# An MLP made layer by layer from seven half-size products, with its activations in DRAM

## What is computed

```
x: (8, 512, 512) fp32;  sa, ca, ga, sb, cb, gb = six rows of C = 512 per batch, from silu(c) @ wmod
h = layernorm(x) * (1 + ca) + sa
x = x + ga * attention(h)                 # 16 heads of 32, causal, W_attn and W_proj
h = layernorm(x) * (1 + cb) + sb
y = relu(h @ W1.T + b1)                   # 512 -> 1024
y = relu(y @ W2.T + b2)                   # 1024 -> 1024
x = x + gb * (y @ W3.T + b3)              # 1024 -> 512
```

## Time and profile before

| | |
|---|---|
| median of three runs | 1615.04 us |
| the profiled execution | 1619.41 us |
| its span, first to last instruction | 1617.6 us |
| attention, to the last matmul and store issue of it | 723.7 us |
| MLP | 893.9 us |
| busy: PE, DVE, ACT, POOL | 95%, 58%, 39%, 27% |
| DRAM traffic, mean | 73 GB/s |

### The profile page before, as it was taken

One profiled execution on the slowest core, in us unless ns is written; L12 is line 12 of the kernel. 1 busy time (PEld: TensorE's weight loads), 2 busy tenths in 40 slices (PEclk: granted clock), 3 DMA queues, 4 the chain that ended last, 5 costly groups with the idle time before them and its releaser, 6 DMA issues.

```text
span 1617.6 us, 31407 instructions
## 1 busy us (share of the span) xinstructions
PE 1540.7 (95%) x12112; PEld 1369.6 (85%) x12112; DVE 938.1 (58%) x2199; ACT 637.5 (39%) x1280; POOL 441.5 (27%) x459
## 2 busy tenths in 40 slices
PE   7899999999999999966899999999999999999998
PEld 6678788878888878855899999999999999999998
DVE  4477877787778777646644444444544444444442
ACT  2166666666666666654312121212121212121221
POOL 2156666666666666660000000000000000000000
PEclk9799999999999999987999999999999999999999
DMA  6534343434343433316201001110111011100100
GB/s 215 151 80 126 87 125 87 126 86 126 87 119 93 119 93 93 93 30 223 94 34 47 27 20 48 46 30 31 34 47 46 2 47 46 40 21 34 46 14 14
DMA packets 80546, 118.33 MB, mean 73 GB/s; under 512 B 10632, under 2 KB 31112, under 8 KB 80400
## 3 DMA queue, kind: packets, MB, share of 16 engines
q1 hardware_dynamic: 72416, 105.19, 24.1%
q10 hardware_dynamic: 7984, 11.03, 1.9%
HBM read 48.52 MB, written 16.81 MB: 40 GB/s over the span
## 4 chain that ended last, share of the span: by engine, by line
PE 52%; DVE 1%; DMA 1%; issue 0%; SPq 0%; ACT 0%; POOL 0%; DVEq 0%; POOLq 0%
PE feature L1268 34%; PE token L1249 17%; PE feature L1239 1%; PE token L1230 1%; DVE w L1180 1%; DMA b_rows<-b 0%; DMA w_ring<-wproj_t 0%; DVE y L1134 0%; SPq L1010 0%; DVE y L1132 0%; ACT w L1086 0%; DVE attn_tiles L1158 0%; POOL mlp_rstd L1047 0%; DVE gated L1170 0%; DVE res_tiles L1145 0%
## 5 line engine op out<-in xcount | busy, mean ns | idle before, releaser
L1268 PE MATMUL feature<-y,w 128*128 128x256 f32 x3072 | 376.2, 283 | 6.5 <-DVE w L1180 6.5
L1268 PEld LDWEIGHTS feature<-y,w 128*128 128x128 f32 x3072 | 372.9, 189 | 8.0 <-DVE w L1180 6.7
L1080 ACT ACTIVATE mlp_full<-feature,b_cols 128x256 f32<-128x256 f32 x256 | 120.1, 474 | 649.5 <-PE feature L1268 561.2
L433 POOL TENSOR_TENSOR prob_lo<-prob,prob_hi 128x512 f16<-128x512 f32 x256 | 297.1, 1165 | 143.4 <-ACT prob L537 142.9
L1132 DVE CAST y<-mlp_full 128x256 fp32r<-128x256 f32 x256 | 75.0, 293 | 304.1 <-ACT mlp_full L1080 303.7
L530 ACT ACTIVATE prob_hi<-key_score 128x512 f16<-128x512 f32 x320 | 191.0, 597 | 134.7 <-PE key_score L828 132.3
L1047 POOL TENSOR_TENSOR mlp_rstd<-mlp_var_eps,mlp_minus_half 128x2 f32<-128x2 f32 x16 | 11.1, 696 | 802.9 <-DVE mlp_var_eps L1153 802.9
L739 PE MATMUL lin<-h_parts,wqkv 128*128 128x512 f32 x768 | 219.5, 410 | 1.1 <-DVE h_parts L582 1.1
L1268 PEld LDWEIGHTS feature<-turned,w 128*128 128x128 f32 x1536 | 188.2, 190 | 8.2 <-DVE w L1180 3.8
L1268 PE MATMUL feature<-turned,w 128*128 128x256 f32 x1536 | 189.4, 283 | 5.8 <-DVE turned L1134 3.4
L537 ACT ACTIVATE prob<-key_score 128x512 f32<-128x512 f32 x320 | 190.5, 595 | 0.0
(11 more groups left out here) (93 smaller groups left out, 1927.6 us busy)
## 6 DMA issues: line engine op xcount, KB each, us to landing
stack<-qk_parts SPq DMA_DIRECT2D x384, 128.0 KB, 2.4
x_tiles<-x SPq DMA_DIRECT2D x32, 256.0 KB, 3.8
attn_dram<-o_rows SPq DMA_DIRECT2D x32, 256.0 KB, 2.3
attn_tiles<-attn_dram SPq DMA_DIRECT2D x16, 512.0 KB, 5.0
res_tiles<-x SPq DMA_DIRECT2D x16, 512.0 KB, 3.5
out<-res_tiles ACTq DMA_DIRECT2D x16, 512.0 KB, 3.0
w_ring<-w_t SPq DMA_DIRECT2D x12, 512.0 KB, 5.6
wmod_sb<-wmod SPq DMA_DIRECT2D x4, 1024.0 KB, 6.3
```

What stands on the lines that cost most here:

```text
L433: nc.gpsimd.tensor_tensor(prob_lo[:, key[1] % 2, u, :], prob[:, u, :], prob_hi[:, key[1] % 2, u, :], ALU.subtract).then_inc(lo_pool, 1)
L1080: nc.scalar.activation(full[:, f % 2, :], fbank[f % 4][:, 0:CH], ACT.Relu, bias=bias[:, f:f + 1])\
L1268: mm = nc.tensor.matmul(fbank[f % 4][:, 0:CH], weights[:, wl, c, f * P:(f + 1) * P], data[:, dl, c, :], start=(c == 0 and i == 0), stop=(c ...
```

## The change

A batch of 512 tokens is a chunk now, and the MLP runs layer by layer: 8 chunks of layer 1 (`expand`, n = 0 to 7), 8 of layer 2 (`middle`, 8 to 15), 8 of layer 3 (`contract`, 16 to 23). In each, both factors are cut into 2 x 2 blocks, and seven products of half-size blocks (s = 0 to 6) take the place of eight. They need sums of blocks: four sums of the data per chunk, made by POOL (`sums`), four of each weight, made once. An operand is then split: high part by ACT (`hi`), rest by DVE (`lo`), into a ring of three buffers, so that operand s is written when product s - 3 is done. The products are added up in PSUM banks and in SBUF by five DVE sums (`second_sum`, `third_sum`, `make_c22`, `make_c21`, `make_c12`; in halves, so ten instructions, in layers 1 and 2). ACT copies product 0 out (`first_product`) and puts bias and ReLU on the four blocks. A block of data is 512 columns per partition in layer 1 and 1024 in layers 2 and 3.

Layer outputs go to DRAM (`y_dram`, four blocks of 512 KB per chunk, issued by ACT in `store_block`) and come back as blocks (`load_block`, by SyncE). The residual rows go to `x2_dram` (1 MB per batch, by SyncE) and come back in `contract` (`load_x2`). In `expand` POOL also adds the gated attention to the rows (`add_rows`) and the third layer's gated bias (`add_bias_rows`), 512 columns each, four per batch. In `contract` DVE multiplies the four output blocks by the gate (`gate`), POOL adds them to the residual (`add_gated`), and SyncE stores halves of the batch (`store_out`); ACT no longer stores `out`. The projection and both turnings of the following batches stand between the products of `expand` (`AUX_AT`). W1, W2 and W3 are loaded and split at the start, at the end of `expand` and at the end of `middle`. All loops are written out.

```diff
--- before.py
+++ after.py
@@ -74,7 +74,8 @@
...
         with ExitStack() as mlp_ctx:
-            mmem = Memory(nc, mlp_ctx)
-            w3 = mmem.sb("w3", [P, 2, NF, C], F32R)
-            weights = ((wproj_t, wproj), (w1_t, w1), (w2_t, w2), (w3_t, w3))
-            mlp(nc, mmem, x, attn_dram, gate_dram, weights, b1_c, b2_c, b3, ident, mod_cols, out)
...
+HB = T // 2
+EXPAND, MIDDLE, CONTRACT = range(3)
+CHUNKS = 3 * B
+STEPS = 7
+K_TILES, M_TILES, BANKS = (2, 4, 4), (4, 4, 2), (2, 2, 1)
+SUMS = ("a", "b", "e", "a", "b", "e", "b")
+FRESH = (True, True, True, False, True, True, False)
...
+AUX_AT = {(0, 3): [(PROJ, 1, 2)], (1, 3): [(PROJ, 1, 3)],
+          (2, 1): [(TURNED, 2, 0)], (2, 3): [(TURNED, 2, 1)], (3, 1): [(TURNED, 2, 2)], (3, 3): [(TURNED, 2, 3)],
+          (5, 1): [(ROWS, 1, 0)], (5, 3): [(ROWS, 1, 1)], (6, 1): [(ROWS, 1, 2)],
+          (6, 3): [(ROWS, 1, 3), (PROJ, 2, 0), (PROJ, 2, 1)]}
...
+W_NEED = [("proj", 0), ("proj", 1)] + [(EXPAND, s) for s in range(STEPS)] \
+    + [(MIDDLE, s, half) for s in (0, 1, 4, 2, 3, 6, 5) for half in range(2)] + [(CONTRACT, s) for s in range(STEPS)]
+W_NO = {item: i for i, item in enumerate(W_NEED)}
...
+    def ring_wait(engine, n, s):
+        if op_no(n, s) >= 3:
+            before = divmod(op_no(n, s) - 3, STEPS)
+            engine.wait_ge(prod_done, done_no(*before, BANKS[layer(before[0])] - 1) + 1)
...
+            def load_block(n, i):
...
+                if n > B:
+                    m = n - 1
+                    if i < 2:
+                        sp.wait_ge(op_sum, sum_no(m, 3) + 1)
+                        sp.wait_ge(op_ready, op_no(m, 0) + 1)
+                    elif i == 2:
+                        sp.wait_ge(op_ready, op_no(m, 3) + 1)
+                    else:
+                        sp.wait_ge(op_ready, op_no(m, 6 if layer(m) < CONTRACT else 5) + 1)
+                elif i >= 2:
+                    sp.wait_ge(op_sum, sum_no(B - 1, 3) + 1)
+                    sp.wait_ge(op_ready, op_no(B - 1, 6) + 1)
+                sp.wait_ge(y_out[i], 16 * (n - B + 1))
+                sp.dma_start(blk[i][:], y_view(n - B, i).rearrange("p (c n) -> p c n", n=HB)).then_inc(blk_in[i], 16)
...
+            def load_x2(k):
+                if k >= 2:
+                    for half in range(2):
+                        sp.wait_ge(out_done[half], 16 * (k - 1))
+                sp.wait_ge(x2_out[k % 2], 16 * (k // 2 + 1))
+                sp.dma_start(x2t[:, k % 2], rows_of(x2_dram, k)).then_inc(x2_in[k % 2], 16)
+            def store_out(k, half):
+                sp.wait_ge(add_done, 4 * k + (4, 3)[half])
+                tiles = slice(2 * half, 2 * half + 2)
+                sp.dma_start(rows_of(out, k)[:, tiles], x2t[:, k % 2, tiles]).then_inc(out_done[half], 16)
+            def contract(n):
+                k = n - CONTRACT * B
+                if k:
+                    store_out(k - 1, 0)
+                if k and k + 1 < B:
+                    load_gate(k + 1)
+                if k + 1 < B:
+                    load_block(n + 1, 0)
+                    load_block(n + 1, 1)
+                if k and k + 1 < B:
+                    load_x2(k + 1)
+                if k + 1 < B:
+                    load_block(n + 1, 2)
+                    load_block(n + 1, 3)
+                store_out(k, 1)
...
+            def add_bias_rows(k):
...
+                for t in range(NT):
+                    nc.gpsimd.tensor_tensor(xt[:, k % 2, t], xt[:, k % 2, t], gb_b3[:], ALU.add).then_inc(xs_ready, 1)
...
+            def sums(n):
...
+                block_wait(pool, n, 1)
+                block_wait(pool, n, 3 if contract_op else 0)
+                if n:
+                    pool.wait_ge(op_ready, op_no(n - 1, 4) + 1)
+                if contract_op:
+                    nc.gpsimd.tensor_tensor(t1, b[1], b[3], ALU.add).then_inc(op_sum, 1)
+                else:
+                    nc.gpsimd.tensor_tensor(t1, b[1], b[0], ALU.subtract).then_inc(op_sum, 1)
+                block_wait(pool, n, 0 if contract_op else 3)
+                ring_wait(pool, n, 1)
+                pool.wait_ge(op_sum, sum_no(n, 0) + 1)
+                if contract_op:
+                    nc.gpsimd.tensor_tensor(low[0], t1, b[0], ALU.subtract).then_inc(op_sum, 1)
...
+                    nc.gpsimd.tensor_tensor(t4, b[2], low[0], ALU.subtract).then_inc(op_sum, 1)
...
+                ring_wait(pool, n, 2)
+                if contract_op:
+                    nc.gpsimd.tensor_tensor(low[1], b[0], b[1], ALU.subtract).then_inc(op_sum, 1)
...
+            def add_gated(n):
...
+                for i, where in enumerate(RELU_ORDER):
...
+                    pool.wait_ge(g_done, 4 * k + i + 1)
+                    nc.gpsimd.tensor_tensor(dst, dst, part(made[where], n, 0).rearrange("p (m n) -> p m n", n=HB),
+                                            ALU.add).then_inc(add_done, 1)
...
+                        add_rows(k + 1, t)
+                    gate_times_b3(k + 1)
                     inverse_deviation(k + 1)
+                    add_bias_rows(k + 1)
+                if k == B - 1:
+                    w2_last_sum()
+                sums(n + 1)
...
+            def contract(n):
+                if n + 1 < CHUNKS:
+                    sums(n + 1)
+                add_gated(n)
...
+            def store_block(n, i):
+                act.wait_ge(relu_done, relu_no(n, i, 3) + 1)
+                act.dma_start(y_view(n, i).rearrange("p (c n) -> p c n", n=512), made[i][:]).then_inc(y_out[i], 16)
...
+                relu(n, C11)
+                if n == B:
+                    w2_hi(6)
+                hi(n, 6)
+                store_block(n, C11)
+                if n == B:
+                    w2_hi(5)
...
+                elif s == 1:
+                    dve.wait_ge(op_sum, sum_no(n, 2) + 1)
+                dve.wait_ge(op_hi, op_no(n, s) + 1)
+                nc.vector.tensor_tensor(op(n, s)[:, 1], whole_value, f32(op(n, s)[:, 0]), ALU.subtract)\
+                    .then_inc(op_ready, 1)
...
+                lo(n, 5)
+                if turn:
+                    turned_lo(k + 2, 3)
...
+                if n == B:
+                    w2_lo(4)
+                lo(n, 3)
+                second_sum(n)
+                if n == B:
+                    w2_lo(2)
+                lo(n, 4)
+                third_sum(n)
+                if n == B:
+                    w2_lo(3)
+                lo(n, 5)
+                if n == B:
+                    w2_lo(6)
+                lo(n, 6)
+                if n == B:
+                    w2_lo(5)
...
+            def contract(n):
+                if n == CONTRACT * B:
+                    make_c12(n - 1)
+                else:
+                    make_c12(n - 1)
+                    gate(n - 1, C12)
+                lo(n, 1)
+                lo(n, 2)
+                lo(n, 3)
+                second_sum(n)
+                lo(n, 4)
+                third_sum(n)
+                lo(n, 5)
+                gate(n, C11)
+                lo(n, 6)
+                make_c22(n)
+                gate(n, C22)
+                if n + 1 < CHUNKS:
+                    lo(n + 1, 0)
+                make_c21(n)
+                gate(n, C21)
...
+            def product(n, s):
+                where, tiles = layer(n), K_TILES[layer(n)]
+                if n % B == 0:
+                    pe.wait_ge(w_ready, W_NO[(where, s, 1) if where == MIDDLE else (where, s)] + 1)
+                pe.wait_ge(op_ready, op_no(n, s) + 1)
...
+                        sum_free(n, s, m // 2)
+                    again = not FRESH[s] or m % 2 == 1
+                    dst = bank_of(n, s, m // 2)[:, m % 2 * HB:m % 2 * HB + HB]
+                    for c in range(tiles):
+                        for i, (wl, dl) in enumerate(TERMS):
+                            begin = FRESH[s] and m % 2 == 0 and c == 0 and i == 0
+                            end = c == tiles - 1 and i == 2
+                            cols = slice(m * P, (m + 1) * P)
+                            if where == CONTRACT:
+                                mm = nc.tensor.matmul(dst, data[:, dl, c, cols], w3[s][:, wl, c, :],
+                                                      start=begin, stop=end, skip_group_check=again)
+                            else:
+                                w = (w1, w2)[where][s]
+                                mm = nc.tensor.matmul(dst, w[:, wl, c, cols], data[:, dl, c, :], start=begin, stop=end,
+                                                      skip_group_check=again)
+                    if m % 2:
...
```

1107 lines of the change are left out of this document (783 added, 324 removed).

## The result

The changed kernel takes 1688.03 us (median of 4 runs, 1683.88 to 1690.07), the kernel before beside it 1615.37: a ratio of 1.044, 95% interval 1.041 to 1.047, slower. The profiled execution's span is 1688.2 us, where the prediction's sum came to 1632.4; the time lies outside its range.

The account below looks back on a forecast made before the run. It took the MLP as PE-bound but for its start: 91.4 us of matmuls saved, overhead 141.8 against 35.6 (+106.2), so +14.8, span 1617.6 to 1632.4; 1630 on the median, range 1585 to 1662.

Parts of the forecast that it names:

- the total of the start: Start of the MLP: product (0,0) and one projection tile done at 793 us, 41 us of overhead against 30.
- the 40.3 us of the middle chunks: Middle: 40.3 us of PE per batch, with POOL's 10.2 and DVE's 15.5 all covered by three operands of lookahead.
- rival 3: Layer 3 matmuls of 256 columns take longer than 0.120 us; at 0.14 it costs 27 us, 1657; chance 0.04.
- the tail: End of the kernel: one PSUM sum, gate, add and store, 6 us of overhead.
- the contract loop: Contract: POOL sums, adds, store, x2 load, block loads, sums again; 31.8 us a turn against 20.2 of PE, 69.9 over six.
- 0.4 us x 7 = 3 us: Expand: `lo` of operand 5, behind one POOL bias-row operation, ends at 22.3 for a product due at 22.0.
- The last sentence of the prediction: Steady gaps in expand or middle, hidden under three operands of lookahead, would make the whole bookkeeping of lateness wrong.
- one cold restart: Contract: PE restarts cold, 2.3 us, counted once in the last chunk and otherwise taken as hidden.
- Rival 2: DVE gets no turn between back-to-back POOL operations; expand +26 us, first contract turn +5, total 1661; chance 0.18.
- The entries: Stage entries: middle's 12 us with lock conflicts, from late w2 splits; contract's 4.5, from POOL's W3 sums ahead of operand sums.
- Rival 1: Contract loop looser than counted, gain survives: 1594 at the port's pace (chance 0.20), 1560 at PE's pace (0.08).
- the port's pace of 25.9: Contract: POOL's 15.3 us and DVE's 10.6 per batch exclude each other on the shared port, more than PE's work.

Follow-up runs that it names:

- one that takes away both: Changed kernel with ScalarE's modulate steps 2 and 3 of the next batch put ahead of the ReLU of block C21: 1654.2 us, ratio 1.023.
- one that takes away the clock's part: Changed kernel with 24 unread matmuls filling PE's idle time before the first projection tile of each expand chunk: 1674.9 us, ratio 1.038.

## Why the prediction was wrong

**Right.** The direction; the total of the start; the 40.3 us of the middle chunks and the 2.88 us of a product in layer 3, so 0.120 us a matmul (rival 3 out); the tail; above all the contract loop, 31.8 a turn against 32.3, and its links: taking the x2 load's wait out gave 2.5 us a turn, taking the store out of the loads' way another 2.

**Luck in two of these.** In the turn, the recorded working has 3.4 MB from 10.5 us on at 389 GB/s, which gives 19.3 and not 21.7; with 19.3 the turn would have been 29.5. Measured from the end of the sums at 1532.5, the adds took 7.9 us in place of 10.0, the last block landed 10.5 us behind the issue of the x2 load in place of 8.7, at 21.7 after all, and four sums took 9.7 in place of 10.2 (1024 columns take 2.36 us, not 2.55). In the start, W1 sums and normalising were through at 767.6, 3.7 us before the 771.3 of the prediction, and the way from there to product 1 took 3.5 us longer than summed: the six W1 splits called hidden took turns with POOL's bias rows up to 789.2, and PE waited 1.19 us for a step behind them.

**The step that failed** is expand, "0.4 us x 7 = 3 us". I had priced one meeting there, POOL's bias rows against `lo` of operand 5, and for the rest trusted that three operands of lookahead cover it. The last sentence of the prediction named that as what would bring it down, and it did. The lookahead covers operands, not the two `aux` banks, and a bank is freed by ACT, in ACT's order, behind a ReLU that waits for DVE, which waits for ACT. The prediction never lists what is queued ahead of `modulate` on ACT. The cost is 3 us of wait a chunk and 2 of clock behind it, 33.8 us in all with chunks 6 and 7: shown by two experiments, one that takes away both and one that takes away the clock's part.

**The clock behind the waits** is a second term at nothing. The sum has one cold restart, 2.3 us in the last chunk (by the earlier trace rows 2.0, and products behind a wait took 1.3 to 2.4 more here), and calls the others hidden. With PE kept warm a chunk of expand lost 2.1 us and a contract turn 1.6.

**Rival 2 gave the right size for a wrong reason.** It had expand chunks of 39 to 40 us, by DVE starving behind POOL's adds. The chunks are 40 us long, but DVE never waits for two of POOL's operations, and the order on ACT alone brings them to 34.9. A symptom that was written down for one mechanism would have been read as its proof.

**The entries** of the stages were sized too small. In `middle(8)` the waits are where and as long as I put them, 3.05, 3.05 and 1.99 us for 3.2, 3.1 and 2.2; the 5.4 us missing are the clock behind them, and the edit that moves the weights forward brought 54.7 us to 45.3. Chunks 6 and 7 took 14 us more than summed. Ahead of product 1 of chunks 7 and 8, where no projection of a further batch fills the time, PE waits 7.34 and 5.58 us for the split of operand 1, and for chunk 7 still 5.46 with the modulation first: POOL's sums can't start before the rows are modulated. For chunk 8, `lo` of operands 1 and 2 took 4.60 us at 1094.67, behind 3.55 of waiting for POOL. Contract's entry was 10.0 us in place of 4.5, as I read it by W3's splits on DVE and not by POOL's sums; of the 7.2 us by which its first turn is longer than PE's work, 3.1 of them priced, 4.6 are a wait for operand 1 again and 1.3 the clock. Apart from the weights' and the modulation's, none of these waits was tested by a run.

**Rival 1, the looser loop,** didn't happen, and the experiments say why the port's pace of 25.9 alone was the wrong thing to look at: with the loads first a turn is 27.8 on average, with PE warm 25.7, so PE's clock was still in it, and moving work off POOL made it longer. DVE and POOL mostly alternate, in expand too, where four bias rows took 5.94 against 5.1 beside two `lo` splits of DVE. The Trainium skill (SBUF — State Buffer, Who interferes with whom) says that whoever issues first holds the shared pair for the whole instruction and the other blocks; the trace agrees on the block, with 2.2 us from one add to the next against 1.28 alone. It doesn't agree that the order of issue decides: at 1045.71 POOL's add was issued first, and three DVE operations issued from 1046.15 on went ahead of it. By the Trainium skill (Trainium Kernel Development and Optimization, Key Constraints) another issuer saves issue time only; here it saved nothing: ScalarE as the second issuer 1688.0, all on SyncE 1682.4, intervals that overlap.

So 91 us of matmuls are gone for 162 us of new overhead (91.4 and the 70.6 between the spans); 73 of these came back by the order of steps within an engine's program and, for the 5.7 that can't be told from the spread, by another issuer of the stores; nothing was added to remove them. Without them the kernel equals the one before, and with PE kept warm it is 0.8% faster.

## What to carry to other kernels

For every buffer that a bottleneck engine waits for, write down who frees it and what is queued ahead of the freeing instruction on that engine; lookahead in one kind of buffer says nothing of another kind. Price an idle stretch of TensorE with what the clock takes behind it: here a wait of 3 us cost 5. In a loop that passes through several engines, look for the link that waits before you move one off it: the busy sum of two engines was neither the bound nor a guide to which move pays.

## What the runs showed of the hardware

A gap of 3.05 us in PE's work was followed by a granted clock of 0.50 over 4 us, and behind one of 5.1 us a product of 24 matmuls took 4.8 us to the next one's start in place of 2.88, its first 4 us at 0.50; the same gap filled with 36 matmuls whose result nobody reads left it at 3.0, at 1.00. With the 24 extra matmuls in expand the projection behind the wait took 5.72 us in place of 8.45. With the loads first the cold restarts of contract were a link of the loop: 1.6 us a turn.

DVE and POOL with all inputs in SBUF exclude each other and mostly take turns operation by operation, however short the one and long the other: a 0.68 us add of DVE took 2.85 beside POOL's sums, and three `lo` splits 7.87 in place of 3.66. Turns aren't kept always: DVE never waited for two POOL operations behind the attention, but one POOL add of 1.28 us took 4.5 while four DVE operations passed.
